# Fourth layer: side programs skip the half-steps of dense attention that hold a value mixing, with paces scaled to the remaining turns

## What is computed

```python
def global_mha(x, in_w, in_b, out_w, out_b, nh):
    q, k, v = qkv_proj(x, in_w, in_b)           # heads of 16
    scores = jnp.einsum('bqhd,bkhd->bhqk', q, k) / np.sqrt(hd)
    attn = jax.nn.softmax(scores, axis=-1)
    o = jnp.einsum('bhqk,bkhd->bqhd', attn, v).reshape(Bq, Sq, D)
    return o @ out_w.T + out_b
x_global = global_mha(x, ...); x_local = local_mha(x, ...)
x_comb = jnp.concatenate([x_global, x_local], axis=-1)
x_fused = silu(x_comb @ fus_w1.T + fus_b1) @ fus_w2.T + fus_b2
x = layer_norm(x + x_fused, gn_g, gn_b)
x_ffn = silu(x @ ffn_w1.T + ffn_b1) @ ffn_w2.T + ffn_b2
x = layer_norm(x + x_ffn, fn_g, fn_b)
```

## Time and profile before

| | us |
|---|---|
| median of 3 runs | 2722.62 (2722.1 to 2729.55) |
| span of the profiled execution | 2761.5 |
| main loop, first to last L2042 matmul | 787.0 |

### The profile page before, as it was taken

One profiled execution on the slowest core, in us unless ns is written; L12 is line 12 of the kernel. 1 busy time (PEld: TensorE's weight loads), 2 busy tenths in 40 slices (PEclk: granted clock), 3 DMA queues, 4 the chain that ended last, 5 costly groups with the idle time before them and its releaser, 6 DMA issues. The chain is left out here.

```text
span 2761.5 us, 25395 instructions
## 1 busy us (share of the span) xinstructions
PE 1840.1 (67%) x8218; PEld 792.3 (29%) x8218; DVE 1628.0 (59%) x3680; ACT 990.0 (36%) x1604; POOL 693.1 (25%) x681
## 2 busy tenths in 40 slices
PE   1574795686489376699788898878888753000099
PEld 1121331222133134466563232222322212000044
DVE  3485767768677776557576665665665512253733
ACT  1242142123204125355305446657655632000033
POOL 2300510340070041044421112332231222574000
PEclk7696787888689688799758989989989865555599
DMA  3301201200120000210010101101000000510020
GB/s 90 84 19 30 61 0 41 52 15 18 29 61 2 23 1 1 73 36 12 34 47 13 39 14 34 39 14 52 23 16 24 4 13 0 100 9 6 24 107 23
DMA packets 58647, 88.68 MB, mean 32 GB/s; under 512 B 18008, under 2 KB 29778, under 8 KB 58266
## 3 DMA queue, kind: packets, MB, share of 16 engines
q1 hardware_dynamic: 48004, 77.66, 9.4%
q10 hardware_dynamic: 6426, 7.99, 1.3%
q0 software_dynamic: 4096, 1.58, 1.2%
HBM read 58.59 MB, written 24.74 MB: 30 GB/s over the span
## 5 line engine op out<-in xcount | busy, mean ns | idle before, releaser
L2351 DVE TENSOR_REDUCE f_half_max<-f_ring 128x1 f32<-128x512 f32 x512 | 339.3, 685 | 294.1 <-PE f_ring L2015 291.6
L2234 ACT ACTIVATE f_probs<-f_ST 128x512 f32<-128x512 f32 x512 | 294.6, 597 | 269.6 <-PE f_ST L2042 266.1
L2015 PE MATMUL f_ring<-f_stacks 96*128 96x512 bf16 x512 | 217.2, 425 | 44.8 <-DVE f_half_max L2351 38.7
L2617 PE MATMUL gm_ps<-xn_cm,x 128*128 128x512 f32 x128 | 62.4, 614 | 274.9 <-PEq L43 274.9
L772 DVE TENSOR_REDUCE att_half_max<-att_ring 128x1 f32<-128x512 f32 x256 | 161.2, 685 | 101.1 <-PE att_ring L659 92.1
L2042 PE MATMUL f_ST<-f_stacks 99*128 99x512 bf16 x512 | 207.9, 411 | 11.8 <-ACT f_probs L2234 11.8
L755 ACT ACTIVATE att_probs<-att_ST 128x1024 f32<-128x1024 f32 x128 | 129.3, 1023 | 155.6 <-PE att_ST L684 155.4
L2061 PE MATMUL f_O<-f_probs,f_v_ext 128*32 128x512 f32 x1024 | 161.2, 706 | 0.1
L3073 POOL DMA_INDIRECT ti_row<-features,slot_from x128 | 125.4, 980 | 56.7 <-issue 38.7
L684 PE MATMUL att_ST<-stacks 96*128 96x512 bf16 (+1 forms) x512 | 137.6, 397 | 0.0
L702 PE MATMUL att_O<-att_probs,v_ext 128*64 128x512 f32 x512 | 131.7, 640 | 6.6 <-DVE att_den L791 6.6
(11 more groups left out here) (553 smaller groups left out, 3538.3 us busy)
## 6 DMA issues: line engine op xcount, KB each, us to landing
f_stacks<-f_parts SPq DMA_DIRECT2D x192, 64.0 KB, 2.2
gates_wide<-gates SPq DMA_DIRECT2D x16, 512.0 KB, 12.5
parts_dram<-l_parts SPq DMA_DIRECT2D x8, 768.0 KB, 4.1
stacks<-parts_dram SPq DMA_DIRECT2D x24, 256.0 KB, 9.7
stacks<-parts_dram ACTq DMA_DIRECT2D x24, 256.0 KB, 10.7
f_parts<-f_parts SPq DMA_DIRECT2D x8, 768.0 KB, 3.4
es_raw<-L_ffn_edge_index SPq DMA_DIRECT2D x8, 512.0 KB, 4.7
bm_mix<-mix SPq DMA_DIRECT2D x8, 512.0 KB, 9.8
```

Of the source, the lines that this page charges most:

```text
L2015: nc.tensor.matmul(ring[:, i % RING], f.stacks[0:STACK, 0, at, t * P:(t + 1) * P], f.stacks[0:STACK, 1, at, n * BANK:(n + 1) * BANK], star ...
L2234: nc.scalar.activation(f.probs[:, s % PROBS, n * BANK:(n + 1) * BANK], ST[:, i % HALVES], ACT.Exp).then_inc(probs_ready, 1)
L2351: nc.vector.tensor_reduce(f.half_max[:, h % 2, t, n:n + 1], ring[:, i % RING], AX.X, ALU.max, negate=True).then_inc(reduced, 1)
```

## The change

A method `half_step(i, visit)` is added to `Beside`. It passes on only half-steps whose remainder by 2 x `VISIT` = 4 isn't 3, and numbers them anew: i = 4t + r becomes turn 3t + r. PE, ACT, DVE and SP call it in place of `turn`. A batch thus has 96 turns; `TURNS` and `LOCAL_START` are set to 96 and 21, the paces to 0.94, 1.06 and 0.83, and the tally's program gets a pace of 0.8. Nothing of the main loop is touched.

```diff
@@ -145,6 +145,12 @@
 
     def __init__(self, *programs):
         self.programs = [[start, start, program] for start, program in programs]
+
+    def half_step(self, i, visit):
+
+        turn, last = divmod(i, 2 * visit)
+        if last != 2 * visit - 1:
+            self.turn(turn * (2 * visit - 1) + last)
 
     def turn(self, now):
         for p in self.programs:
@@ -1660,11 +1666,12 @@
     AHEAD = 2
     MOVES = 2 * SHARE * NC2
     LOADS, LOAD_AFTER = 12, 8
-    TURNS = 2 * STEPS
+    HALF_STEPS = 2 * STEPS
+    TURNS = HALF_STEPS - HALF_STEPS // (2 * VISIT)
     X0_USES = 19
     PRE_USES, LOCAL_USES = 8, 22
-    LOCAL_START = 28
-    PRE_PACE, LOCAL_PACE, TAIL_PACE = 1.25, 1.42, 1.1
+    LOCAL_START = 21
+    PRE_PACE, LOCAL_PACE, TAIL_PACE, TALLY_PACE = 0.94, 1.06, 0.83, 0.8
     WINDOW, LOCAL_HEADS = 5, 4
     ROWS = WINDOW * LOCAL_HEADS
     EARLY, EARLY_TALLIES, LATE, LATE_TALLIES, LATE_TURNS = 128, 5, 96, 4, 28
@@ -1828,7 +1835,7 @@
         programs = [(0, pre(0))] + ([] if first is None else [(0, first())])
         head = len(programs)
         if tally is not None:
-            programs.append((0, tally()))
+            programs.append((0, paced(tally(), f.TALLY_PACE)))
         programs.extend((0, other()) for other in others)
         for b in range(B):
             if b + 1 < B:
@@ -2080,7 +2087,7 @@
                 scores_transposed(s, n)
                 if n == NC2 - 1 and s >= lag and (s - lag) % VISIT == 0:
                     mix((s - lag) // VISIT)
-                beside.turn(NC2 * s + n)
+                beside.half_step(NC2 * s + n, VISIT)
         for v in range((len(steps) - lag + VISIT - 1) // VISIT, len(steps) // VISIT):
             mix(v)
         beside.finish()
@@ -2237,7 +2244,7 @@
                     for group in range(all_groups - 1):
                         if s == last_step(group) + VISIT:
                             carry_off(group)
-                beside.turn(i)
+                beside.half_step(i, VISIT)
         carry_off(all_groups - 1)
         beside.finish()
 
```

## The result

The changed kernel takes 2741.45 us (median of four runs, 2737.79 to 2745.43) against 2724.65 us (2722.1 to 2729.55) before: a ratio of 1.0057, 95% interval 1.0039 to 1.0075. It is slower by 16.8 us where 11 us of gain were forecast, and lies above the stated range.

A forecast was written before the change was run, and what follows sets the result against it. The prediction took the loop to be bound by hand-overs between PE, DVE and ACT, none of them full. Its terms -19 + 6 + 2 = -11 us took 2722.6 to 2711.6 us, with a range of 2695 to 2737.

The forecast's parts named there:

- What bounds the loop: Fourth layer's attention loop, 789 us: no engine full, bound by how PE, DVE and ACT hand over through shallow buffers.
- The sum: Whole kernel: -19 + 6 + 2 = -11 us, from 2722.6 to 2711.6 us, ratio 0.996.
- The signs: Loop: no side matmul beside mixing, mixing intervals near 1.6 us, loop 776 us, DVE idle down 11; wrong above 2.15.
- rival 1: Plain half-steps: uncovered DVE work decides at 0.93 us per step, +14 us, 2736 us; chance 0.15.
- -19 us for PE's steps: Mixing half-steps: 54 PE side steps leave, saving 0.35 us each because DVE starves less; bounds 11 and 29 us.
- Rival 2: Loop: the gap only moves, -11 with +6 and +2 gives -3 us, 2720 us; chance 0.24.
- +6 us for DVE's and ACT's steps: Mixing half-steps: 35 DVE steps leave at 0.18 us each, ACT's cost nothing; bounds -4 and 33 us.
- +2 us for steps that come closer: Side programs: new paces bring turns together, as pre's second transposes on turn 8, so PE waits; bounds 0 and 11 us.
- The tally of batch 0 at 0 us: Batch 0: tally's DVE steps spread over 126 half-steps in place of 118, same sum, nobody waits: 0.
- SP, POOL and what lies behind the loop at 0: SP's transfers at nearly the same half-steps, POOL not paced, the tail of batch 3 not paced: 0 each.
- The rule against the change: Score tiles in PSUM: skill's rule on consistent bubbles makes the two-tile ring the cause, so moving steps only moves the gap.
- The clock: Loop: denser waits lengthen the lower clock level, up to 16 us of PE work, net +13, 2736 us; chance 0.08.

The follow-up runs named there:

- e1: Kernel before, with all engines holding side steps back in the mixing half-steps (slipping to the next), at old paces: 2726.2 us, ratio 0.9990.
- e8: Kernel before, with ACT and DVE holding side steps back at i % 4 = 1, where nothing is mixed: 2749.8 us, ratio 1.0100.
- e9: Kernel before, with only PE holding side steps back at i % 4 = 1, where nothing is mixed: 2700.9 us, ratio 0.9919.
- e10: Kernel before, with PE alone doing side steps due in a mixing half-step one half-step earlier: 2748.3 us, ratio 1.0093.
- e15: Kernel before, with only the local branch, on all engines, in the half-steps where the change puts it: 2712.3 us, ratio 0.9944.
- e6: Changed kernel, with the tally's steps put in the half-steps they have in e1: 2736.1 us, ratio 1.0032.
- e12: Kernel before, with every side step of PE one half-step later and nothing held back: 2685.8 us, ratio 0.9848.
- e17: Kernel before, with the local branch in the change's half-steps and PE's side steps one half-step later: 2706.7 us, ratio 0.9930.
- e4: Kernel before, with only ACT holding side steps back in the mixing half-steps, slipping to the next: 2748.3 us, ratio 1.0078.

## Why the prediction was wrong, step by step

**What bounds the loop** was read rightly, as engines that wait for each other. But I read the gaps by interval and by engine pair, and not by what PE did next. PE's gaps ahead of side matmuls were 59.9 of its 123.2 us of idle time, nearly half; the prediction names one kind of them (L1844) and prices all of them at 2 us.

**The sum.** It failed in two steps of about equal size. Leaving the mixing half-steps was to bring -19 + 6 = -13 us and brought -1.3 (e1, where all engines are held back and nothing is paced anew). Steps that come closer were to cost +2 and cost 15.3, from e1 to the change as the times stand, 18.1 against each one's own runs of before.

**The signs** that the prediction named: there is no side matmul beside a mixing, but mixing intervals are 1.80 us and not 1.6, the loop is 797 us and not 776, and DVE's idle time before its maxima didn't fall by 11 (280.3 us in the table of waits, before 277.5). Plain intervals with side work, at 2.10 us, stayed under the 2.15 that were to refute it. The sign of rival 1, over 148 us of PE waiting for DVE's maxima, is barely met (150.5 in the same table, for PE's weight loads), and it took e8 to refute that rival.

**-19 us for PE's steps.** Held alone, PE gains 23.1 us, close to the term; but the reason was false. The prediction put it on a DVE that starves behind 2.30 us of mixing and side work. e9 gains as much with as many side steps at the mixing as before (54), and e10, which clears them all, loses 27.5. The step that failed is the comparison of intervals with and without a side matmul: steps at i % 4 = 3 stand among other steps than those at 0, 1 and 2, and a mean over unlike neighbours isn't the price of moving one. That -19 lies near 23.1 is luck; and the change doesn't hold PE alone, so even the measured 23.1 isn't a term of it. Rival 2, that moving the side matmuls only moves the gap, had the right result for this part (e1).

**+6 us for DVE's and ACT's steps.** Measured 27.6 with PE left in place, and 22.3 for ACT alone, which I had at nothing. Here the failed step is the kind of cost. I priced an uncovered instruction; what costs is a reader or producer that comes later while PE's next matmul stays where it was. e8 has that cost in full (29.0 us) with all cover kept. Rival 1 had the right sign and, with +14 against the measured +16.8, nearly the right size, by the wrong mechanism.

**+2 us for steps that come closer.** This term was mis-sized: from e1 to the change, where only the steps' integer places differ, the time rises by 15.3 us. The prediction followed one pair of steps (pre's transposes) and took the rest as unchanged because 0.94 x 4/3 is 1.253. The average spacing did stay; single distances didn't. By the yields, ACT's copy out of the bank and PE's next of the six projections are 2, 2, 2, 1 and 1 half-steps apart in before, 3, 2, 1, 2 and 1 in e1 and 1, 1, 2, 1 and 1 in the change, and PE's gaps ahead of the six are 9.0, 7.7 and 17.2 us. I had read L1906's idle time and not used it; L1873's I had not read. But steps that come closer aren't the whole of it. Over both banks the distances are nearly those of before (22 of 47 at one half-step or none, before 21), and e15 has the six projections just as close and gains 13.3 us. What the runs show is that the new places cost when all are taken together; which meetings make up the 15 us stays open.

**The tally of batch 0 at 0 us.** It costs 5 us at most (e6). Batch 0 grew by 9 us, 5 or 6 more than batches 1 and 2. In it PE was busy 5.0 us longer, 194.5 us against 189.5, with the same 1053 matmuls at a clock of 0.82 against 0.87; in batch 3, at 0.92 against 0.89, it was busy 6 us less.

**SP, POOL and what lies behind the loop at 0.** Right: from the last L2042 matmul to the end are 488.5 us in after and 491.1 in the second profile of before.

**The rule against the change.** The Trainium skill, page Perfetto Trace Analysis, section Optimization Strategy, says of gaps to determine "what is blocking execution by identifying the semaphore or semaphores it's waiting on", and to make those dependencies start sooner. I used the section's other sentence, on bubbles and buffers. The runs bear this one out in part: PE's wait before L1906 for L2314 is 6.8 us in before and 1.0 in e12, DVE's for scores falls by 71 us, and no buffer was added. Whether a third score tile would have done the same was not tried. And finding such waits does not give their price: e17 has little more of PE's side gaps than e12 (21.2 us against 16.8) and is 20.9 us slower.

**The clock** as a rival had 0.08. In the runs the time at the lower level goes mostly with the length of the loop (113 us in the two fastest kernels, 256 in the slowest), but not always: e4 loses 22 us at 161. Which way cause and effect run was not tested. The change itself has 14 to 21 us more of it, at half rate worth at most about 10 us of its 16.8; as PE's busy time over the loop didn't grow, no such cost is seen in its profile.

## What to carry to other kernels

Where engines work through hand-placed steps in order, look first at the distance of a step to the one that feeds it or empties its bank: count, per pair, how many of the main loop's turns lie between, and read PE's idle time by the instruction that it stands in front of. Here, holding all engines' steps at the mixing alike changed nothing that could be told (e1), moving PE against the others by one turn gained 1.5%, and by two turns lost 1.2%. The gain of one turn was not the same everywhere (39.8 us on before, 5.6 on e15), so measure it on the placing at hand; moving all engines by one turn, as a control, was not run. When paces are scaled, compare the integer places of the steps on each engine, across all programs that share it, since equal averages hide new meetings; and test a gain that is put down to a place with a control at another place.

## What the runs showed that I had not expected

- Delaying one quarter of PE's side steps by one half-step gives 0.8% at either of two places (0.9918, 0.9919), delaying all of them 1.5%, and by two half-steps -1.2%.
- Effects of placing don't add up: 22.3 and 18.8 us alone are 27.6 together, and 39.8 and 13.3 us of gain together leave 18.4.
- The lower clock of the loop went from 113 to 256 us with nothing but the order of the same instructions.
